# Attention scores of a head pair: one zero-padded 128-row product per head, or two 64-row products on separate row tiles

## The reference, cut to what matters

```python
qkv = shift_token(x) @ wqkv
q, k, v = to_heads(...)                      # 8 heads of 64
q, k = rotary_xpos(l2norm(q) * qs, l2norm(k) * ksc)
sim = jnp.einsum('bhwid,bhwjd->bhwij', bq, bk)   # windows w of 128 queries, 256 keys
attn = jax.nn.softmax(jnp.where(mask, -big, sim), axis=-1)
out = jnp.einsum('bhwij,bhwjd->bhwid', attn, bv)
x = x + out @ wo
h = layernorm(shift_token(x)) @ w1 + b1;  a, g = split(h)
x = x + (a * gelu(g)) @ w2 + b2
```

## Time and profile before

| | |
|---|---|
| median of 3 runs | 855.98 us (854.7 to 859.11) |
| span of the profiled execution | 855.5 us |
| PE busy (products) | 782.2 us, 91% |
| PE weight loads | 700.8 us, 82% |
| DVE / ACT / POOL busy | 570.1 / 505.5 / 443.9 us |
| score products, L577 + L581 | 45.6 + 74.5 us busy |
| mean granted TensorE clock | 0.970 |

### The profile page before, as it was taken

How to read it: one execution, slowest core, us unless ns; L and a number is a source line. 1 busy time by engine, 2 the same in 40 slices (tenths; PEclk the granted TensorE clock), 3 DMA queues, 4 the chain that set the end, 5 groups by cost and what they waited for, 6 DMA issues and landing times. The chain is left out here.

```text
span 855.5 us, 17687 instructions
## 1 busy us (share of the span) xinstructions
PE 782.2 (91%) x5088; PEld 700.8 (82%) x5088; DVE 570.1 (67%) x1675; ACT 505.5 (59%) x1241; POOL 443.9 (52%) x626
## 2 busy tenths in 40 slices
PE   5988777989999999999998998999999999999977
PEld 4877556978888888888887887888888888888866
DVE  3788896385848484848485856657575758585842
ACT  2333436366767676666667574757575757575742
POOL 2433464373838383838383646637373737373722
PEclk9999987799999999999999998999999999999998
DMA  6444424051000000000000001010101010101000
GB/s 205 131 140 143 121 45 148 6 217 36 3 31 7 28 9 27 10 25 12 21 15 22 16 2 50 2 49 0 49 0 49 0 49 0 49 0 38 1 26 13
DMA packets 31156, 38.34 MB, mean 45 GB/s; under 512 B 7356, under 2 KB 21776, under 8 KB 31120
## 3 DMA queue, kind: packets, MB, share of 16 engines
q1 hardware_dynamic: 31120, 37.90, 13.8%
HBM read 29.51 MB, written 8.39 MB: 44 GB/s over the span
## 5 line engine op out<-in xcount | busy, mean ns | idle before, releaser
L1351 POOL TENSOR_SCALAR pr<-pr,rl 128x128 f32<-128x128 f32 (+1 forms) x256 | 106.5, 429 | 106.1 <-DVE rl L1128 104.4
L839 ACT ACTIVATE pr<-sm,nb,rn 128x128 f32<-128x128 f32 (+1 forms) x256 | 137.6, 539 | 24.3 <-DVE nb L1123 23.2
L1119 DVE CUSTOM_DVE_ANT_0 sm<-ps,wmask 128x128 f32<-128x128 f32 (+1 forms) x256 | 81.3, 355 | 60.4 <-ACT pr L839 27.4
L415 PE MATMUL ps<-hT_hi,w_hi 128*128 128x256 f32 (+1 forms) x384 | 111.0, 289 | 1.4 <-DVE hT_lo L1090 1.4
L415 PE MATMUL ps<-hT_hi,w_lo 128*128 128x256 f32 (+1 forms) x384 | 108.4, 282 | 0.0
L415 PE MATMUL ps<-hT_lo,w_hi 128*128 128x256 f32 (+1 forms) x384 | 108.1, 281 | 0.0
L1314 POOL TENSOR_TENSOR rn<-ss,nhalf 128x16 f32<-128x16 f32 x32 | 95.3, 2977 | 3.7 <-POOL ss L1310 2.0
L796 ACT ACTIVATE sqb<-ps 128x512 f32<-128x512 f32 x64 | 38.2, 598 | 85.5 <-PE ps L415 85.5
L415 PE MATMUL ps<-wqkv_hi,yT_hi 128*128 128x512 f32 x192 | 80.6, 420 | 8.8 <-DVE arena L966 5.4
L1256 POOL TENSOR_SCALAR hrs<-hmv 128x2 f32<-128x2 f32 x16 | 3.1, 193 | 150.2 <-DVE hmv L1144 150.2
L606 PE MATMUL ps<-pT,vz 128*128 128x256 f32 x256 | 80.3, 396 | 0.2 <-DVE oT_lo L1111 0.2
(11 more groups left out here) (147 smaller groups left out, 2284.6 us busy)
## 6 DMA issues: line engine op xcount, KB each, us to landing
arena<-x SPq DMA_DIRECT2D x16, 256.0 KB, 3.7
ystream<-arena SPq DMA_DIRECT2D x16, 256.0 KB, 2.0
y_next<-ystream SPq DMA_DIRECT2D x16, 256.0 KB, 2.9
y_res<-ystream SPq DMA_DIRECT2D x16, 256.0 KB, 2.7
arena<-L_ffn_w SPq DMA_DIRECT2D x2, 1364.0 KB
arena<-ctx SPq DMA_DIRECT2D x8, 256.0 KB, 4.0
arena<-mask_BxSxS_ik SPq DMA_DIRECT2D x8, 256.0 KB, 2.8
xmid<-arena SPq DMA_DIRECT2D x8, 256.0 KB, 2.0
```

Of the source, the lines that this page charges most:

```text
L415: last = mm(out, lhsT(a), rhs(b), start=(start and i == 0), stop=(stop and i == 2))
L839: A(pr[:, h % NS, a:b], sm[:, h % NS, a:b], ACT.Exp, bias=nb[:, h, t:t + 1], scale=rn8[:, t, h:h + 1], accum_out=ls[:, h, t:t + 1]).then_i ...
L1119: V.tensor_tensor_reduce(sm[:, h % NS, a:b], bank(h % NS)[:, a:b], wmask[:, a:b], 1.0, NEG, ALU.add, ALU.max, mx[:, h, t:t + 1]).then_inc( ...
L1351: G.tensor_scalar(pr[:, h % NS, a:b], pr[:, h % NS, a:b], rl[:, h, t:t + 1], 1.0, ALU.mult, ALU.mult).then_inc(pn_done, 1)
```

## The change

The queries are kept in `qT`, laid out as the keys are, without zeros. A head's score product takes only its own 64 rows of `qT` and `kT`, rows 0 to 63 for the even head and 64 to 127 for the odd one. Both heads of a pair are issued together. PE's order changes with it: heads 0 and 1 before the five `down`, heads 2 and 3 at h = 0, heads 4 and 5 at h = 2, heads 6 and 7 at h = 4. `queries_T` is one ACT copy of 128 rows in place of two of 64, and the memset of `qz` goes.

```diff
-        qz = sb("qz", [P, HEADS, S])
+        qT = sb("qT", [P, PAIRS, S])
...
-                def scores_own(h):
-
-                    if h >= NS:
-                        pe.wait_ge(mx_done, T * (HEADS * s + h - NS + 1))
-                    mm(bank(h % NS)[:, 0:P], qz[:, h, 0:P], kT[:, h // 2, 0:P], start=True, stop=True)
-
-                def scores_both(h):
-
-                    mm(bank(h % NS)[:, P:3 * P], qz[:, h, P:S], kT[:, h // 2, :], start=True, stop=True)\
-                        .then_inc(s_mm2, 1)
+                def scores_own(pair):
+
+                    for h in (2 * pair, 2 * pair + 1):
+                        if h >= NS:
+                            pe.wait_ge(mx_done, T * (HEADS * s + h - NS + 1))
+                    for h in (2 * pair, 2 * pair + 1):
+                        r = slice(h % 2 * DH, h % 2 * DH + DH)
+                        mm(bank(h % NS)[:, 0:P], qT[r, pair, 0:P], kT[r, pair, 0:P], start=True, stop=True)
+
+                def scores_both(pair):
+
+                    for h in (2 * pair, 2 * pair + 1):
+                        r = slice(h % 2 * DH, h % 2 * DH + DH)
+                        mm(bank(h % NS)[:, P:3 * P], qT[r, pair, P:S], kT[r, pair, :], start=True, stop=True)\
+                            .then_inc(s_mm2, 1)
...
-                    pe.wait_ge(q_done, 2 * T * s + 2)
+                    pe.wait_ge(q_done, T * s + 1)
                     pe.wait_ge(k_done, T * s + 1)
                     pe.wait_ge(v_done, T * (s + 1))
-                    for h in range(NS):
-                        scores_own(h)
-                    pe.wait_ge(q_done, 2 * T * (s + 1))
+                    scores_own(0)
+                    pe.wait_ge(q_done, T * (s + 1))
                     pe.wait_ge(k_done, T * (s + 1))
-                    for h in range(NS):
-                        scores_both(h)
+                    scores_both(0)
...
                     for h in range(HEADS + 1):
-                        if h + NS < HEADS:
-                            scores_own(h + NS)
-                            scores_both(h + NS)
+                        if h % 2 == 0 and h + 2 < HEADS:
+                            scores_own(h // 2 + 1)
+                            scores_both(h // 2 + 1)
...
-                    q = qz[:].rearrange("p (c j) n -> p c j n", j=2)
-                    for j in range(2):
-                        lo = j * DH
-                        A(q[lo:lo + DH, :, j, t * P:(t + 1) * P],
-                          ps[lo:lo + DH, i, :].rearrange("p (c n) -> p c n", c=PAIRS), ACT.Copy)\
-                            .then_inc(q_done, 1)
+                    A(qT[:, :, t * P:(t + 1) * P], bank(i).rearrange("p (c n) -> p c n", c=PAIRS),
+                      ACT.Copy).then_inc(q_done, 1)
...
-                    for part in (qz, vz):
-                        G.memset(part[:], 0.0).then_inc(zeros_set, 1)
+                    G.memset(vz[:], 0.0).then_inc(zeros_set, 1)
...
-ZEROS = 8
+ZEROS = 7
```

## The result

The changed kernel takes 908.22 us (median of 4 runs, 907.28 to 909.24), the kernel before 855.86 (4 runs): ratio 1.0592, 95% interval 1.056 to 1.0623, slower. The forecast was 904 us, within 885 to 922. The profiled execution spans 905.5 us, 50.0 more than before.

The account below looks back on a forecast made before the run. PE was taken as full in the heads loop, with ACT nearly so and order-sensitive queues. Late scores +51 us, memset -1.75 and query copy -1.5 gave +48: span 903.5, median 904 us, range 885 to 922.

Parts of the forecast that it names:

- The order decides: Heads loop: later-issued scores(4,5) and (6,7) delay DVE, POOL and PE in turn; +3.2 us a step, 51 over 16 steps.
- The ring's turn: Heads loop: pair's scores, row_max, row_sum, normalise(3), tr_probs(3), weighted(2), then next pair's scores; one cycle 4.3 to 4.5 us.
- Row_max(4): DVE's row maximum of head 4 in the heads loop: starts at 685.57 where it was 682.79, 2.8 us later.
- The step's period: Length of a steady step in the profile after: 46 to 47 us in place of 43.05.
- The cost of a pair: Two heads' score products on PE: 1.3 us, overlap saving 0.2, switches taking back 0.34; ends 0.65 and 2.03.
- the emptied pipe: PE going between whole and split array: up to 0.17 us a switch, 0.34 for two switches a pair.
- The play of the queues: Four compute queues played through from the first wide product: `y_next` transposes +3.2 us a step, between +2.16 and +4.2.
- The clock: Rival, heads loop: PE's new waits drop an eighth of each loop to 1.2 GHz, +28 us, 932 us; chance 0.05.
- the main case: Whole kernel: late scores in the heads loop decide, with or without overlap; 904 us, own range 887 to 920, chance 0.85.
- The memset: Cross-attention stage: without POOL's `qz` memset two DVE copies end earlier, -1.75 us once, or 0 if input load is late.
- The query copy: One ACT copy of 128 rows for two of 64: about 0.1 us back in 15 steps, -1.5 us.
- The rivals of the other signs: Heads loop: array's relief decides, 832 us, chance 0.06; lost and won time cancel, within 0.5% of 856, chance 0.04.

Follow-up runs that it names:

- e1_padded_new_order: The kernel before, zero-padded queries, memset and two query copies kept, with only PE's score order taken from the change, no row tiles: 904.75 us, ratio 1.0519.

## Why the prediction was right, and by what errors

**The order decides: right, and shown.** The padded kernel in the new order loses 5.2%, the tiled kernel with two pairs moved up a turn gains 1.1%. DVE's waits of 2.39 and 2.22 us and PE's of 0.69 to 0.74 stand where the prediction had put them. The ring's turn was put at 4.3 to 4.5 us and measures 4.47. Row_max(4) was played at 2.8 us later than before, counted from the first wide product; it is (722.28 - 713.89) - (682.79 - 676.72) = 2.3 later. The step's period was put at 46 to 47 us and is 45.5 at full clock.

**The cost of a pair: mechanism half right, the term too large.** I took 1.3 us, on the ground that only neighbours overlap and weight loads go one at a time. The four narrow instructions of a pair take 0.33 us and the four wide ones 0.53, against 0.45 and 0.86 in series (`e1_padded_new_order`): the same as for one head in split mode, 0.32 and 0.53. So both tiles, their loads too, run fully side by side, and the load rate read from one-column products is no bound for loads to different tiles. Nor do the instructions run as the program orders them, first both of one head and then both of the other, from which the prediction had only neighbours overlap: in the trace they go in twos, one of each head, 6 to 7 ns apart. The second head's first wide product starts with the first head's first, not with its second.

The pair costs 0.65 us and the switches 0.34, in all 1.0. The 0.34 is the figure that I had named for the emptied pipe, but it came so by luck: the trace has it in four parts, two of them around the first loads. That I offset it with an overlap of 0.2 instead of 0.65 was the error in this term.

The Trainium skill (TensorE: Matmul & The Clock Gate, Part 3) has the products of different row tiles start a few ns apart; the trace agrees, with 6 to 7 ns. The Trainium skill (TensorEngine Tiling (Array Packing), Key Properties) says that changing the tiling mode drains TensorE; the trace agrees in so far as going in and out costs 0.34 us.

**The play of the queues: too high by itself.** The padded kernel in the new order has no switch and a pair of 1.31 us, for which the play gave +3.16 us. From the first wide product to the `y_next` transposes it is 2.8 us longer than before. So of the 0.7 us between the 3.2 forecast for a step and the 2.5 measured, about 0.4 is the play's own error and the rest the pair's. Over 16 steps that is 40 us in place of 51. Which of its terms was too large was not found: it has scores(4,5) 0.15 us too late in that kernel and the transposes 0.3.

**The clock: a rival at 0.05 that came true beside the main case.** I set it against the steady step's own 1 us waits at clock 1.00. The loop of the changed kernel has several such waits close together (0.98, 0.69, 0.74 and 0.74 us), and in half of the steady steps the clock went from 2.4 to 1.2 GHz for a while. It cost 8 to 10 us where I had priced it at 28. So the closeness of 904 to 908 owes something to luck: the main case by itself was forecast at 904 and is 896 to 900 (1.0471 times the 855.86 of before, and the 899.54 measured with filled waits), too high by 4 to 8, and the clock, which the 904 left out, made up for that.

**The memset: right.** Forecast -1.75, the copies gave 1.74 (3.42 - 1.68), and the start of step 0 is some 1.6 earlier. **The query copy: wrong by little.** -1.5 forecast, 0 measured. DVE's 0.29 us wait was not what set the start of the scores. In the changed kernel the wide ones wait 0.36 us for the copy of the transposed keys (713.89).

**The rivals of the other signs** needed row_max(4) in time; the early pairs show what they would have been: even then 8 to 9 us, not 24, since a pair saves 0.3 us net of its switches.

Left open: why the clock fell in one steady step and not in the next, which by their rows are alike, and whether split products have a part in it. The padded kernel in the new order kept its clock, but its two later waits are 0.46 us and not 0.74.

## What to carry to other kernels

When a change makes a unit of work larger (a pair in place of a head), look first at where the larger unit is issued in each queue, and play the queues through: here the array's saving was 0.3 us a pair, and the place in the queue cost 2.5 us a step and turned to a gain when two pairs moved up one turn. A split array pays for each visit (0.34 us here), so it wants both tiles filled each time; one head at a time the kernel lost 2.2%, a part of it to a lower clock in step 0. And PE when made to wait may lose its clock too: price a new wait on PE above its own length. Last, a forecast that adds up can hide errors that cancel: run the main term alone, as the padded kernel does here, before trusting the sum.

## What was not expected of the hardware

Fp32 products of two 64-row tiles overlap in full, weight loads included: four wide instructions take 0.53 us, the time of two. A visit to split mode costs 0.09 us ahead of it, 0.10 between its first two products (the first load starts with its product, where before it started 0.11 us ahead), 0.09 behind it and 0.05 at the next transpose. And the clock fell in six of twelve steady steps of the tiled kernel, but in none of the padded kernel with the same order, whose later waits are shorter; filling the waits with idle products removed it.
